# A two-layer cross-attention kernel: context and dequantized weight split in natural layout and turned by DMA, V projected before K on six banks, row constants added in the last stage

## The chip, the cores and the metric

The kernel runs on one NeuronCore of a Trainium2 chip. The time is the device time of one execution in microseconds (us). The engines are TensorE (PE in the rows; PEld is its weight load), VectorE (DVE), ScalarE (ACT), GpSimd (POOL) and SyncE (SP), which only issues transfers. Each runs its own list of instructions in order and waits at semaphores. PSUM has eight banks of 128 x 512 float32.

## What is computed

x is 2 x 512 x 1024 (eight tiles of 128 tokens), the context 2 x 1024 x 1024 (sixteen tiles). Four residual steps, each on a layer norm of x:

```python
x = x + tanh(g_xattn[0]) * matmul(fake_quant(ln(x)), fake_quant(ctx))            # A
x = x + tanh(g_ffn[0])   * (quant_per_token(ln(x)) @ dequant(W_int, scale).T + bias)  # B
x = x + tanh(g_xattn[1]) * attention(ln(x), ctx, ctx, Wq, Wk, Wv) @ Wo           # 32 heads, 8 K/V heads of 32
x = x + tanh(g_ffn[1])   * (ln(x) @ dequant_fp4(packed, scales).T)               # F
```

fake_quant(v) is (clip(round(v/s + z), 0, 255) - z) * s. Step A is done on integers shifted by 128, exact in float16; the two zero points come back as a term per token (c1, from the row sums of the quantized x) and a term per column (c2, from the column sums of the quantized context). A term that is constant along a row drops out of every later layer norm.

The K, V, Q and output projections work in float32 accuracy: each factor is split into a float16 high part and a float16 rest, and three products are summed (hi*hi, hi*lo, lo*hi).

## The kernel before, in words

**Stage 1, chunks.** The context is taken in four chunks of four tiles. A tile is loaded into one of four slots `cx`; TensorE turns it in float32 (`ctx_turn`, line 1264, eight 128 x 128 transposes into banks 0 and 1); ScalarE copies the turned halves to float16 (`ctx_high`, line 616), VectorE subtracts (`ctx_low`, line 899). GpSimd scales and clips the same slot for step A (`ctx_affine`, lines 451 and 453), VectorE rounds it into `r2` (`ctx_round`, line 905), which frees the slot for SP's next load. On TensorE a chunk c has two K projections (`k_proj`, 24 matmuls of 128 x 512 each) and four V projections (`v_proj`, 24 of 128 x 256) on banks 4 and 5 alone, and between them the turns of chunk c + 1, two turns of W's rows (`wd_turn`, into banks 2 and 3, with `wd_high`, `wd_low`), and the row sums c1 (`c1_sum`, line 1288, on bank 7). Beside it runs the first layer norm of two x tiles a chunk: statistics and affine on VectorE, `ln1_affine`, `ln1_round`, `ln1_out` between ScalarE and VectorE through one buffer y and one buffer r16, which SP turns by a DMA transpose (`xt1`, line 282). GpSimd adds c1 to x after it (`add_c1`, line 459, two tiles after each of the chunks 1, 2 and 3, the last two at the end), then c2 (`add_c2`, line 464).

**Stage 2, A and B.** `AB_OPS` sets the order: a0 to a4, b0, a5, b1, a6, b2, a7, b3 to b7, each on one of three pairs of banks. VectorE adds the product to x and takes statistics, ScalarE and VectorE quantize per token, SP turns the result (`xt2`, line 286). SP's list has two loads of Wq ahead of xt2(0), and they wait for GpSimd (`wq_low`, line 485), which comes to that after `add_c2` of all eight tiles. The third layer norm's scale and shift come in two groups of four tiles (`ln3_affine`).

**Stage 3, Q.** ScalarE writes the normalized tile and its high part (`y3_out`), GpSimd the rest, SP turns both (`xt3`, lines 290 and 292). Q is projected for batch 0 (eight blocks), then for batch 1, interleaved with the first score maxima (line 1410). In between VectorE unpacks the fp4 weight eight times (`unpack`, line 1139) into the one buffer r16, which SP turns into `w2T` (`w2_turn`, line 337); `q_low` (line 1124), for which TensorE's next Q block waits, stands behind it in VectorE's list.

**Stage 4** is the attention of 16 K/V groups; **stage 5** the output projection and step F, with stores from x.

## Time and profile before

| | us |
|---|---|
| median of 3 runs (lowest, highest) | 961.75 (957.26, 962.38) |
| the profiled execution's own time | 963.96 |
| its span, first to last instruction | 962.0 |
| TensorE busy | 859.1 (89% of the span) |
| VectorE, ScalarE, GpSimd busy | 595.2, 443.0, 556.5 |
| mean granted TensorE clock | 0.966 |

A busy share is a mean over stages. The stages lie as follows in the span, by TensorE's instructions: stage 1 from 24.3 us (its first projection) to 170.8, stage 2 to 267.7, stage 3 to 389.5, stage 4 to 818, stage 5 to the end. In stages 4 and 5 the change touches one thing only, the constant c1.

### The profile page before, as it was taken

Reading aid. Unit: us, or ns where it says so; the run is one execution under the profiler, and the core shown is the slowest. Engines: PE = TensorE matmul, PEld = TensorE weight load, DVE = VectorE, ACT = ScalarE, POOL = GpSimd, SP = SyncE. Lnnn points to the kernel's source line nnn. Section 1 sums busy time; section 2 is a strip of 40 time slices with the busy share of each in tenths; the row PEclk is TensorE's granted clock in tenths of the full one; section 3 lists DMA queues with packets and bytes.
Section 4 is the critical chain, followed back from the end, with each engine's and each line's share of the span. In section 5 each row is a group of like instructions: output and inputs, shape, how many; then the busy total and the mean of one; then the engine's idle time right before and its main releaser. Section 6 shows DMA issues by size and latency. Waiting matters only on the chain.

```text
span 962.0 us, 14337 instructions
## 1 busy us (share of the span) xinstructions
PE 859.1 (89%) x4592; PEld 341.2 (35%) x4592; DVE 595.2 (62%) x842; ACT 443.0 (46%) x740; POOL 556.5 (58%) x244
## 2 busy tenths in 40 slices
PE   3976779869985789799999999999999998999998
PEld 2645456424432334222222222222222221444443
DVE  4754365798823365577778777777778760155522
ACT  3343333544632110376667766777767767011000
POOL 4316246984635331178888888888888888321200
PEclk9998979979997989799999999999999999999999
DMA  4961522343377651144455445554445444222242
GB/s 171 359 175 37 161 56 76 88 105 93 61 185 148 181 142 44 53 91 98 94 118 118 96 102 113 118 118 107 101 98 109 101 88 82 50 44 44 55 131 76
DMA packets 102649, 103.09 MB, mean 107 GB/s; under 512 B 67152, under 2 KB 87632, under 8 KB 98512
## 3 DMA queue, kind: packets, MB, share of 16 engines
q1 hardware_dynamic: 98000, 68.97, 26.2%
q0 software_dynamic: 4608, 33.56, 17.3%
q8 instruction: 27, 0.44, 0.2%
q14 instruction: 14, 0.11, 0.0%
HBM read 41.55 MB, written 12.58 MB: 56 GB/s over the span
## 4 chain that ended last, share of the span: by engine, by line
PE 55%; DVE 16%; DMA 6%; issue 6%; POOL 4%; DVEq 4%; ACT 3%; POOLq 2%; SPq 2%; ACTq 1%
PE sbank L1456 10%; PE sbank L1465 10%; PE mpair L1410 9%; DVE mx L1152 5%; DVEq L857 3%; PE sbank L1542 3%; PE sbank L1557 3%; PE sbank L1546 3%; PE sbank L1559 3%; PE sbank L1544 3%; PE sbank L1297 3%; PE sbank L1298 3%; PE sbank L1299 3%; DMA regK<-r 2%; POOL X L464 2%
## 5 line engine op out<-in xcount | busy, mean ns | idle before, releaser
L1152 DVE TENSOR_REDUCE mx<-mpair 128x1 f32<-128x1024 f32 x256 | 301.3, 1216 | 82.1 <-PE mpair L1410 81.9
L803 ACT ACTIVATE regC<-sbank 128x512 f32<-128x512 f32 x512 | 279.5, 595 | 129.6 <-PE sbank L1456 128.0
L1456 PE MATMUL sbank<-regD 98*128 98x512 f16 x512 | 179.6, 388 | 9.3 <-DMA regD<-mT 5.1
L1410 PE MATMUL mpair<-regD 96*128 96x512 f16 x512 | 157.0, 384 | 7.8 <-DVE mx L1152 3.2
L553 POOL TENSOR_TENSOR wraw<-regC 128x2048 f32<-128x2048 f32 x32 | 145.2, 4537 | 24.5 <-ACT regC L803 12.4
L1465 PE MATMUL sbank<-regC,regD 128*32 128x512 f32 x1024 | 137.2, 608 | 1.0 <-ACT regC L803 1.0
L1456 PEld LDWEIGHTS sbank<-regD 98*128 98x128 f16 x512 | 46.6, 97 | 202.0 <-ACT regC L803 164.3
L553 POOL TENSOR_TENSOR regD<-regC 128x2048 f32<-128x2048 f32 x16 | 72.8, 4551 | 52.9 <-ACT regC L803 52.8
L553 POOL TENSOR_TENSOR tail<-regC 128x2048 f32<-128x2048 f32 x16 | 76.7, 4795 | 0.8 <-ACT regC L803 0.8
L1410 PEld LDWEIGHTS mpair<-regD 96*128 96x128 f16 (+1 forms) x512 | 49.3, 99 | 59.9 <-DVE mT L1162 10.6
L1297 PE MATMUL sbank<-xT_hi,regC 128*128 128x512 f16 x128 | 51.5, 403 | 20.3 <-DVE tail L1124 15.9
L459 POOL TENSOR_SCALAR X<-X,c 128x1024 f32<-128x1024 f32 x8 | 29.6, 3700 | 49.3 <-ACT c L646 49.3
L483 POOL TENSOR_SCALAR wraw<-wraw 128x1024 f32<-128x1024 f32 x16 | 17.2, 1075 | 64.9 <-ACT regR L746 31.3
L1298 PE MATMUL sbank<-xT_lo,regC 128*128 128x512 f16 x128 | 51.3, 401 | 0.0
L1299 PE MATMUL sbank<-xT_hi,regC 128*128 128x512 f16 x128 | 51.2, 400 | 0.0
L591 POOL TENSOR_TENSOR tail<-y,r 128x1024 f16<-128x1024 f32 x8 | 17.0, 2126 | 56.4 <-ACT r L844 56.4
L1264 PE MATMUL mpair<-id,xT_lo 128*128 128x128 f32 x128 | 22.1, 330 | 30.8 <-DVE regC L899 26.6
L1542 PE MATMUL sbank<-regR,xT_hi 128*128 128x512 f16 x128 | 48.5, 379 | 0.0
L1557 PE MATMUL sbank<-regK,xT_hi 128*128 128x512 f16 x128 | 48.5, 379 | 0.0
L1544 PE MATMUL sbank<-regR,xT_hi 128*128 128x512 f16 x128 | 48.5, 379 | 0.0
L1546 PE MATMUL sbank<-regR,xT_lo 128*128 128x512 f16 x128 | 48.5, 379 | 0.0
L1559 PE MATMUL sbank<-regK,xT_lo 128*128 128x512 f16 x128 | 48.5, 379 | 0.0
(165 smaller groups left out, 1318.3 us busy)
## 6 DMA issues: line engine op xcount, KB each, us to landing
regD<-wraw POOLq DMA_DIRECT2D x16, 1024.0 KB, 7.0
tail<-wraw POOLq DMA_DIRECT2D x16, 1024.0 KB, 7.0
xT_lo<-in_ctx SPq DMA_DIRECT2D x16, 512.0 KB, 5.4
wraw<-in_L_ffn_W_int SPq DMA_DIRECT2D x8, 512.0 KB, 6.5
wraw<-in_L_xattn_Wq SPq DMA_DIRECT2D x8, 512.0 KB, 3.7
wraw<-in_L_xattn_Wo SPq DMA_DIRECT2D x8, 512.0 KB, 4.1
regD<-q_hi_scratch SPq DMA_DIRECT2D x32, 128.0 KB, 2.5
out<-X SPq DMA_DIRECT2D x16, 256.0 KB, 2.0
```

Source lines behind the costliest of these rows:

```text
L553: nc.gpsimd.tensor_tensor(p_sum[pr if pr < 3 else 1][:, :, :], probs[:, (2 * pr) % 4, :, :], probs[:, (2 * pr) % 4 + 1, :, :], ALU.add).th ...
L803: nc.scalar.activation(probs[:, kt % 4, h, :], bank[4 + h % 2], ACT.Exp, scale=SCALE).then_inc(s["exp_ok"], 1)
L1152: v.tensor_reduce(mx[m][:, bass.ds(n, 1)] if par is not None else mx[m][:, n:n + 1], slot[:, :, :], AX.XY, ALU.max).then_inc(s["mx_red"], 1)
L1297: pe.matmul(dst, whi(k), xhi(k), start=(k == 0), stop=False)
L1298: pe.matmul(dst, whi(k), xlo(k), start=False, stop=False)
L1299: m = pe.matmul(dst, wlo(k), xhi(k), start=False, stop=(k == KD - 1))
L1410: m = pe.matmul(mpair[slot][:, half, :], qst[par][0:96, bass.ds(n * P, P)], kst[par][0:96, half * 512:(half + 1) * 512], start=True, stop= ...
L1456: pe.matmul(bank[4 + h % 2], kst[par][0:98, kt * P:(kt + 1) * P], qst[par][0:98, h * 512:(h + 1) * 512], start=True, stop=True).then_inc(s ...
L1465: m = pe.matmul(bank[6][HD * h:HD * h + HD, :], vst[par][:, kt * HD:(kt + 1) * HD], probs[:, kt % 4, h, :], start=(kt == 0), stop=(kt == K ...
L1542: pe.matmul(bank[4 + h], xT_hi[:, k, bass.ts(t, P)], wo_hi[:, k, h * H2:(h + 1) * H2], start=(k == 0), stop=False)
L1544: pe.matmul(bank[4 + h], xT_hi[:, k, bass.ts(t, P)], wo_lo[:, k, h * H2:(h + 1) * H2], start=False, stop=False)
L1546: m = pe.matmul(bank[4 + h], xTl[:, k, bass.ts(t, P)], wo_hi[:, k, h * H2:(h + 1) * H2], start=False, stop=(k == KD - 1))
```

## The change

- **Context.** The tile is split where it lies, in natural layout: `ctx_high` is one 128 x 1024 copy to float16 on ScalarE, `ctx_low` one 128 x 1024 subtraction on VectorE, into two buffers each (`nat_hi`, `nat_lo`, in the room of X tiles 6 and 7). SP turns both by DMA transposes (`ctx_turn`, 32 in all). GpSimd's scaling of a slot waits for `ctx_lo`.
- **W.** After `wd_scale` the same: high part on ScalarE, rest on GpSimd, two buffers, 16 DMA transposes (`wd_turn`). Chunk 1 has one W tile, chunk 2 two, the last chunk five.
- **Projections.** TensorE has nothing else in stage 1 but V on banks 0 to 3, then K on banks 4 and 5, and in the last chunk the column sums (banks 6 and 7).
- **c1.** The row sum is a by-product of `ln1_out` (`accum_out`), all eight constants come from one small VectorE instruction, ScalarE adds them to x behind `y_high` in stage 5 (lines 942 and 943), and `f_out` waits for that (`x_c1`). The matmuls of `c1_sum` and GpSimd's `add_c1` are gone. `add_c2(t)` waits until the first layer norm has read tile t.
- **Start.** Wv is loaded ahead of Wk; the six scalars are loaded from ScalarE's queue. X tiles 6 and 7 are loaded only when the last context transpose has landed.
- **Stages 2 and 3.** Four groups of two tiles in `ln3_affine`; y3 of tiles 0 to 5 ahead of the first Q block, 6 and 7 behind blocks 0 and 1. `unpack` has two buffers (`w2b`), and the first waits for the transposes of tiles 4 to 7 instead of 0 to 3.

```diff
+            def ctx_turn(u):
+                cols = bass.ds((u // TB % 2) * 512 + (u % TB) * P, P)
+                if u >= 2 * TB:
+                    sp.wait_ge(s["kv_mm"], 6 * (u // TB - 1))
+                sp.wait_ge(s["ctx_hi"], u + 1)
+                sp.dma_start_transpose(ctxT_hi[:, :, cols], nat_hi[u % 2]).then_inc(cth[u % 2], 16)
+                sp.wait_ge(s["ctx_lo"], u + 1)
+                sp.dma_start_transpose(ctxT_lo[:, :, cols], nat_lo[u % 2]).then_inc(ctl[u % 2], 16)
+
+            def wd_turn(w):
+                if w == 0:
+                    sp.wait_ge(s["wkv_lo"], 4)
+                sp.wait_ge(s["wd_hi_ok"], w + 1)
+                sp.dma_start_transpose(wd_hi[:, :, bass.ts(w, P)], wnat_hi[W_BUF[w]]).then_inc(wdh[W_BUF[w]], 16)
+                sp.wait_ge(s["wd_lo_ok"], w + 1)
+                sp.dma_start_transpose(wd_lo[:, :, bass.ts(w, P)], wnat_lo[W_BUF[w]]).then_inc(wdl[W_BUF[w]], 16)
+                if w < KD - 2:
+                    load_wint(w + 2)
 
...
+            for c in range(NCH - 1):
+                u = TB * (c + 1)
+                ctx_turn(u)
+                if c == 0:
+                    load_ctx(7)
+                else:
+                    store_k(c - 1)
+                ctx_turn(u + 1)
+                if c == 0:
+                    load_wint(0)
+                    load_wint(1)
+                    sp.dma_start(X[:, 2:4, :], x_v[:, 2:4, :]).then_inc(x_in[1], 16)
+                if u + TB < U:
+                    load_ctx(u + TB)
+                ctx_turn(u + 2)
+                if c > 0:
+                    wd_turn(c - 1)
+                if u + TB < U:
+                    load_ctx(u + TB + 1)
+                store_v(c)
+                ctx_turn(u + 3)
+                if u + TB < U:
+                    load_ctx(u + TB + 2)
                 xt1(2 * c)
-                if c < NCH - 1:
-                    store_v(c)
-                    next_wint(c)
-                else:
-                    for k in range(2):
-                        sp.wait_ge(s["wd_tr"], 2 * (KD - 2 + k) + 2)
...
+            store_k(NCH - 2)
+            wd_turn(3)
+            wd_turn(4)
+            store_v(NCH - 1)
+            wd_turn(5)
+            xt1(T - 2)
+            wd_turn(6)
+            load_w(wq_v, 0, 0)
+            wd_turn(7)
+            load_w(wq_v, 1, 1)
+            xt1(T - 1)
+            store_k(NCH - 1)
```


ScalarE and VectorE in a chunk, TensorE's list and the last stage:

```diff
+            def ctx_high(u):
+                act.wait_ge(cin[u % TB], 16 * (u // TB + 1))
+                if u >= 2:
+                    act.wait_ge(cth[u % 2], 16 * (u // 2))
+                    act.wait_ge(s["ctx_lo"], u - 1)
+                nc.scalar.activation(nat_hi[u % 2], cx[:, u % TB, :], ACT.Copy).then_inc(s["ctx_hi"], 1)
...
+            def chunk(c, first=False):
+                u = TB * (c + 1)
+                ctx_high(u)
+                v_out(c, 0, first)
+                ctx_high(u + 1)
+                ln1_root(c)
+                v_out(c, 1, first)
+                ctx_high(u + 2)
+                if c > 0:
+                    wd_high(c - 1)
+                v_out(c, 2, first)
+                ln1_affine(2 * c)
+                v_out(c, 3, first)
+                ctx_high(u + 3)
+                ln1_out(2 * c)
+                if c == 2:
+                    wd_high(2)
+                ln1_affine(2 * c + 1)
                 k_out(c, 0, first)
-                ctx_part(0)
-                ln_sd(2 * c, 2, s["ln1_stat"], c + 1, s["ln1_sd"])
-                if not first:
-                    c1_out(2 * c - 2)
+                ln1_out(2 * c + 1)
                 k_out(c, 1, first)
-                if not first:
...
+            def ctx_low(u):
+                dve.wait_ge(s["ctx_hi"], u + 1)
+                if u >= 2:
+                    dve.wait_ge(ctl[u % 2], 16 * (u // 2))
+                v.tensor_tensor(nat_lo[u % 2], cx[:, u % TB, :], nat_hi[u % 2], ALU.subtract).then_inc(s["ctx_lo"], 1)
+
...
+            def chunk(c):
+                u = TB * (c + 1)
+                ctx_low(u)
                 if c == 1:
                     dve.wait_ge(x_in[1], 32)
-                stats(2 * c, 2 * c)
-                stats(2 * c + 1, 2 * c + 1).then_inc(s["ln1_stat"], 1)
-                d()
-                round_part(0)
+                ln1_stats(c)
+                ctx_low(u + 1)
+                if c > 0:
+                    wd_scale(c - 1)
+                ctx_round(u)
+                ln1_affine(c)
+                ctx_low(u + 2)
+                ctx_round(u + 1)
+                ln1_round(2 * c)
+                if c == 2:
+                    wd_scale(2)
+                ctx_low(u + 3)
+                ctx_round(u + 2)
+                k_low(c, 0)
+                ln1_round(2 * c + 1)
...
                 nc.scalar.activation(y_hi, y[:, :], ACT.Copy).then_inc(s["y_hi"], 1)
+                if first:
+                    act.wait_ge(s["c1_ok"], 1)
+                nc.scalar.activation(X[:, t, :], X[:, t, :], ACT.Identity,
+                                     bias=c1[:, bass.ds(t, 1)]).then_inc(s["x_c1"], 1)
```


```diff
                 else:
-                    dve.wait_ge(s["w2_tr"], 16 * w)
-                dst = r16[:, :].rearrange("p (b j e) -> p b j e", b=NB4, e=2)
+                    if w >= 2:
+                        dve.wait_ge(w2_tr[w % 2], 16 * (w // 2))
+                dst = w2b[w % 2].rearrange("p (b j e) -> p b j e", b=NB4, e=2)
                 for e in range(2):
...
+            dve.wait_ge(xt3_hi[1], 16 * TB)
+            dve.wait_ge(xt3_lo[1], 16 * TB)
             for n in range(6):
                 unpack(n, n == 0)
                 q_low(0, n + 2, n % 2)
...
             for c in range(NCH):
-                chunk(c, first=(c == 0), more=(c < NCH - 1))
+                for j in range(TB):
+                    v_proj(c, j)
+                if c == NCH - 1:
+                    c2_sum(0)
+                    c2_sum(1)
+                k_proj(c, 0)
+                if c == NCH - 1:
+                    c2_sum(2)
+                    c2_sum(3)
+                k_proj(c, 1)
 
```


How this moves instructions. First ScalarE, one chunk (c = 1) before; regC is the turned context, regD the turned W, tail the K pair, r the quantized x, X and vtmp as named:

```order
L653 ACTIVATE tail<-sbank 128x512
L616 ACTIVATE regC<-mpair 128x4x128 x2
L627 ACTIVATE sd<-mv,sc 128x2
L646 ACTIVATE c<-sbank,sc 128x1
L653 ACTIVATE tail<-sbank 128x512
L646 ACTIVATE c<-sbank,sc 128x1
L616 ACTIVATE regC<-mpair 128x4x128 x2
L659 ACTIVATE vtmp<-sbank 128x8x32
L634 ACTIVATE y<-X,bb,rr 128x1024
L616 ACTIVATE regC<-mpair 128x4x128 x2
L622 ACTIVATE regD<-mpair 128x4x128 x2
L659 ACTIVATE vtmp<-sbank 128x8x32 x2
L641 ACTIVATE r<-y,sc 128x1024
```


and after (X now holds the split context, tail also the split W):

```order
L682 ACTIVATE X<-xT_lo 128x1024
L722 ACTIVATE vtmp<-mpair 128x8x32
L682 ACTIVATE X<-xT_lo 128x1024
L695 ACTIVATE sd<-mv,sc 128x2
L722 ACTIVATE vtmp<-mpair 128x8x32
L682 ACTIVATE X<-xT_lo 128x1024
L691 ACTIVATE tail<-wraw 128x1024
L722 ACTIVATE vtmp<-mpair 128x8x32
L702 ACTIVATE y<-X,bb,rr 128x1024
L722 ACTIVATE vtmp<-mpair 128x8x32
L682 ACTIVATE X<-xT_lo 128x1024
L709 ACTIVATE r,c<-y,sc 128x1024
L702 ACTIVATE y<-X,bb,rr 128x1024
```


Between two chunks' first casts stood the copies out of the turns; now each cast is a single instruction ahead of the V copies (line 722), and `ln1_out` of the chunk before (the line-709 row that follows a K copy) stands ahead of the next chunk's first cast.

Second SP, the same chunk before:

```order
L221 DMA xT_lo<-in_ctx 128x1024 x3
L261 DMA k_hi_scratch<-tail 128x2x512
L262 DMA k_lo_scratch<-tail 128x2x512
L221 DMA xT_lo<-in_ctx 128x1024
L282 DMA_TRANSPOSE xT_hi<-r 128x8x128
L268 DMA v_scratch<-vtmp 128x8x128
L234 DMA wraw<-in_L_ffn_W_int 128x1024 x2
L282 DMA_TRANSPOSE xT_hi<-r 128x8x128
```


and after, the start of it:

```order
L254 DMA_TRANSPOSE regC<-X 128x8x128
L238 DMA xT_lo<-in_ctx 128x1024
L252 DMA_TRANSPOSE regC<-X 128x8x128
L254 DMA_TRANSPOSE regC<-X 128x8x128
L260 DMA_TRANSPOSE regD<-tail 128x8x128
L262 DMA_TRANSPOSE regD<-tail 128x8x128
L245 DMA wraw<-in_L_ffn_W_int 128x1024
L238 DMA xT_lo<-in_ctx 128x1024
L277 DMA v_scratch<-vtmp 128x8x128
L252 DMA_TRANSPOSE regC<-X 128x8x128
L254 DMA_TRANSPOSE regC<-X 128x8x128
L238 DMA xT_lo<-in_ctx 128x1024
```


On SP's queue stand eight context transposes and two of W for each chunk beside the two of x (line 285), in one list with the loads.

Third SP in stage 3, before, from the load of Wo to the second turn of the unpacked weight (regK is its turned form, r the buffer); lines 332 and 333 store Q, lines 350 to 355 stage a K/V group:

```order
L278 DMA wraw<-in_L_xattn_Wo 128x1024 x2
L337 DMA_TRANSPOSE regK<-r 128x8x128
L332 DMA q_hi_scratch<-tail 128x512
L333 DMA q_lo_scratch<-tail 128x512
L350 DMA regD<-q_hi_scratch 32x4x512 x2
L350 DMA regD<-q_lo_scratch 32x4x512
L353 DMA regD<-k_hi_scratch 32x1024
L353 DMA regD<-k_lo_scratch 32x1024
L353 DMA regD<-k_hi_scratch 32x1024
L355 DMA regD<-v_scratch 128x256
L337 DMA_TRANSPOSE regK<-r 128x8x128
```


and after, from the same load to the same turn (lines 387 and 388 store Q):

```order
L281 DMA wraw<-in_L_xattn_Wo 128x1024 x2
L387 DMA q_hi_scratch<-tail 128x512
L388 DMA q_lo_scratch<-tail 128x512
L392 DMA_TRANSPOSE regK<-r 128x8x128
L387 DMA q_hi_scratch<-tail 128x512
L388 DMA q_lo_scratch<-tail 128x512
L392 DMA_TRANSPOSE regK<-regD 128x8x128
```


Between the first two turns of the unpacked weight stood a store of Q and the seven loads of a staging; now stands one store, and the two turns read two buffers, r and regD.

## Rows read from the trace of the kernel before

**Rows 1.** windows: us, busy (instructions) of each engine, clock, DMA share, GB/s
```profile
24.30:55.20 30.90, 29.02 (x193) 19.79 (x194) 21.27 (x36) 15.22 (x25) 11.30 (x9) 1.00 0.81 294
55.20:97.80 42.60, 29.24 (x209) 21.01 (x209) 20.46 (x37) 13.88 (x27) 17.09 (x10) 0.92 0.38 112
97.80:140.90 43.10, 31.60 (x208) 21.86 (x208) 20.45 (x37) 13.67 (x27) 16.85 (x10) 0.84 0.38 104
140.90:170.80 29.90, 29.89 (x208) 19.38 (x209) 16.09 (x27) 12.35 (x22) 18.21 (x7) 1.00 0.32 84
170.80:200.50 29.70, 18.02 (x98) 8.06 (x96) 25.07 (x42) 14.71 (x17) 28.69 (x12) 0.88 0.48 117
200.50:267.70 67.20, 67.15 (x304) 29.98 (x304) 56.14 (x97) 33.00 (x32) 41.62 (x23) 0.98 0.35 80
267.70:331.40 63.70, 46.45 (x193) 19.87 (x194) 20.87 (x34) 17.22 (x20) 24.10 (x14) 0.87 0.69 170
331.40:389.50 58.10, 51.85 (x225) 22.26 (x222) 32.85 (x39) 8.67 (x12) 13.58 (x9) 0.94 0.35 98
```

**Rows 2.** what TensorE waited for, 0 to 260 us: total, times, longest
```profile
PE mpair L1264 <- DVE regC L899: 26.6, 5, 7.9
PE mpair L1390 <- DMA xT_hi<-r: 10.2, 1, 10.2
```

**Rows 3.** timeline, stage 1: start, us, engine, line, operation, [idle before]
```profile
38.81 0.27 PE L1297 MATMUL sbank<-regK,regC 128*128 128x256 f16 x1
...
41.44 1.04 PE L1264 MATMUL mpair<-id,xT_lo 128*128 128x128 f32 x8
...
64.38 1.15 ACT L641 ACTIVATE r<-y,sc 128x1024 f16<-128x1024 f32 x1 [8.84 <-DMA xT_hi<-r]
...
71.51 7.40 POOL L459 TENSOR_SCALAR X<-X,c 128x1024 f32<-128x1024 f32 x2 [17.91 <-ACT c L646]
...
81.32 0.69 DVE L905 TENSOR_SCALAR regR<-xT_lo 128x1024 f16<-128x1024 f32 x1 [10.48 <-POOL xT_lo L453]
...
83.72 1.54 DVE L911 SCALAR_TENSOR_TENSOR wraw<-wraw,wscale 128x1024 f32<-128x1024 int32 x1
...
88.40 1.22 DVE L911 SCALAR_TENSOR_TENSOR wraw<-wraw,wscale 128x1024 f32<-128x1024 int32 x1
```

**Rows 4.** groups by line and form, 0 to 200 us: busy us, mean ns, idle
```profile
L464 POOL TENSOR_TENSOR X<-X,xT_lo 128x1024 f32<-128x1024 f32 x8 | 21.0, 2654 | 0.3
...
L888 DVE SCALAR_TENSOR_TENSOR regK<-regD,regK 128x1024 f16<-128x1024 f32 x4 | 5.3, 1323 | 3.0 <-ACT regK L606 3.0
...
L485 POOL TENSOR_TENSOR regC<-wraw,regC 128x1024 f16<-128x1024 f32 x2 | 4.3, 2126 | 0.3
...
L606 ACT ACTIVATE regK<-regD 128x1024 f16<-128x1024 f32 x4 | 4.2, 1055 | 4.3 <-DMA regD<-in_L_xattn_Wv 2.8 <-DMA regD<-in_L_xattn_Wk 1.5
```

**Rows 5.** landing of line 282's transposes; two on SP's queue; DMA from 58.2 to 69.0
```profile
DMA to landing us min/median/max: 3.1/4.6/6.1
...
262.65 1.33 SPq L292 DMA_TRANSPOSE xT_lo<-regR  x1
264.03 1.33 SPq L290 DMA_TRANSPOSE xT_hi<-regR  x1
...
GB/s 137 273 341 379 372 383 379 421 432 311 319 319 217 326 250 157 111 89 260 295 329 343 355 341 338 425 381 455 455 349 425 440 455 349 342 273 199 59 289 143
DMA packets 4201, 3.38 MB, mean 313 GB/s; under 512 B 2224, under 2 KB 3760, under 8 KB 4201
```

**Rows 6.** what TensorE, then VectorE waited for, 250 to 410 us
```profile
PE sbank L1297 <- DVE tail L1124: 15.9, 3, 10.1
PE sbank L1297 <- DMA xT_lo<-regR: 4.4, 1, 4.4
...
DVE r L1139 <- DMA regK<-r: 33.5, 5, 12.7
```

**Rows 7.** the page's 40 slices of the span: ACT
```profile
ACT  3343333544632110376667766777767767011000
```

641 lines of the change are left out of this document (309 added, 332 removed).

## The prediction

> **What bounds the kernel now.** I read the windows first [rows 1]: chunks 1 and 2 of stage 1 take 42.6 and 43.1 us, and in them no engine is full: TensorE 29 and 32 us, VectorE 20, GpSimd 17, the transfers 0.38. A V projection takes 41.44 - 38.81 = 2.63 us [rows 3], K with twice the columns 5.2, so four V and two K need 21 us; the rest of TensorE's time is turns, row sums and the lower clock. Where nothing is full, a circle of waits sets the pace, and the waits show it. TensorE's turns of the context waited 26.6 us for VectorE's subtraction [rows 2]. VectorE stood 10.5 us ahead of a rounding, for GpSimd; GpSimd had spent 7.4 us on two additions of c1, and had waited 17.9 us for that c1; ScalarE had stood 8.8 us for the one buffer r to be turned [rows 3]. So c1 (x quantized, turned, summed, added) delays the next chunk's context and with it K's store and the next projection.
>
> Stage 2 is TensorE's from 200.5 on: 67.15 busy of 67.2 us [rows 1]. Ahead of it b0 stands 10.2 us for its transposed tile [rows 2]. Stage 3 takes 63.7 + 58.1 = 121.8 us [rows 1] for 16 blocks of 5.2 and 16 score products of two matmuls, some 7 us together: 90. The other 32 are waits and slow clock (0.87 and 0.94 granted): TensorE waited 15.9 us for `q_low` and 4.4 for the transposes of y3, and `q_low` stood behind `unpack`, which waited 33.5 us for the one buffer r [rows 6].
>
> **Stage 1 after.** Out of TensorE go the turns of context and W and the row sums; 21 us a chunk are left, so TensorE stops being near the bound. Out of GpSimd go eight additions of 3.7 us, 29.6 us. What comes in is 48 DMA transposes on SP's queue. In a row they are issued 1.38 us apart [rows 5]; alone one lands in 3.1 to 6.1 us, median 4.6 [rows 5]. Each brings 256 KB, 190 GB/s at 1.38 us. The trace doesn't show many of them among loads. Bounds: 0.7 us, if they ran like a plain load of that size in its best moments (0.256 MB at some 380 GB/s), and 2.2 us: from 58.2 to 69.0 us the transfers moved 3.38 MB with two of them, and if the other 2.86 MB went at the 455 GB/s of the best slice, 6.3 us, the two had 4.5 [rows 5]. I take 1.4, the row that is nearest.
>
> The Trainium skill (Advanced Engine Details and Errata, section X-Bar Transpose (TRN2)) says that such transposes are as fast as regular DMAs, 350 to 400 GB/s; the 1.38 us of this trace contradict it by a factor of two. By that rule the circle below would be some 5 us shorter, which is the low rival.
>
> Is it bandwidth or a circle? A middle chunk now moves 12 transposes (8 context, 2 W, 2 x) of 1.4, and loads and stores of 3.5 MB, some 10 us at 350 GB/s: 27 of transfer time. The circle is longer. From the first cast of a chunk to the next chunk's: cast 1.1 (line 606's 1.055 for 128 x 1024 [rows 4]); then VectorE's list up to the third subtraction: subtraction 1.3 (line 888 [rows 4], the nearest two-input pass), statistics 3.1 (four of 0.7 and the sums, an estimate), subtraction 1.3, W scaling 1.2, rounding 0.7, affine 3.2 (88.40 - 83.72 less the 1.5 of the W scaling [rows 3]), subtraction 1.3: 12.1. Then SP: the third tile's low turn 1.3, W's high turn 1.3, the wait for GpSimd's rest of W (line 485, 2.1 [rows 4]), 4.7 in all; W's low turn, two loads, V's store, the fourth tile's two turns, a load: 5.5; then the transpose of x, issued behind some 5 us of transfers: 8 to landing. ScalarE's `ln1_out` of the second x tile waits for that, because r is one buffer, and it stands ahead of the next chunk's first cast: 1.2, and K's copy 0.6. Sum 33.2 us, against 43 now. DVE and ACT passes of the new forms I price by these rows though no row shows two SBUF operands with a float16 result at 128 x 1024 but line 888; between 1.1 and 1.7 each.
>
> Start: the first V projection now needs one tile's turns and Wv. A V at 19 us (between 13, if nothing stood in the queue, and today's 24.3); the fourth V waits for tile 3's turns and ends at 34. Then a circle a chunk: the last V of chunk 3 ends at 34 + 3 x 33 = 133. Behind it: column sums 3.5, K 5.2, a wait of 7 for ScalarE's copy of the column sums (in its list behind W's casts and the layer norm of x tiles 6 and 7, whose load now starts last), sums 3.5, K 5.2, and 1.6 of clock: a0 at 159, today 170.8.
>
> From a0 to b0 today 29.7 us. After: GpSimd has six tiles of `add_c2` left at 2.65, W's last rest 2.1 and two `wq_low` of 3.3 ([rows 4], line 485 and its scaling), ahead of which SP doesn't issue xt2(0); that ends near 185, then issue and landing 4.6: b0 at 190, today 200.5. Gain at b0: 10 us. From there TensorE is full as today. VectorE gets two more `ln3_affine` of some 3.5 us, and has 67.2 - 56.1 = 11 us free [rows 1], so I cost that at nothing; without the cover it would be 3.
>
> **Stage 3 after.** y3 of tiles 0 to 5 comes while TensorE runs b4 to b7 (27 us), so the 4.4 us wait and some 2.4 us at the lower clock behind it go. Then the new wait: `unpack` now stands for tile 7. From Q's start: block 1 ends at 10.4, y3(7) 2.4, rest 2.1, turns 4.6: 20; unpack 2.3 and `q_low` 0.7 (estimates by line 888): 23. Block 4 could start at 20.8: 2.2 us of wait in place of the 10.1 us one [rows 6]. After that a turn of w2 is issued on its own buffer two blocks (10 us) ahead of its use, and lands in 5: no wait. Of today's 32 us some 5 stay: gain 27.
>
> **Stage 5.** Eight additions of c1 on ScalarE, 1.2 us each, where ScalarE is at 0 to 1 tenths [rows 7]; a tile there takes over 10 us. Nothing. If ScalarE's adding to a sum in `ln1_out` costs, it is within 0.5 us a tile, 1 a chunk.
>
> **Sum.** 10 + 27 = 37 us off the profiled execution's own 963.96: 927. The median of the runs lies 2.2 lower, so 925.
>
> **Rivals.**
> - *Transposes slow beside loads (the other side).* At 2.2 us each, 12 a chunk: the queue alone is 12 x 2.2 + 10 = 36 us, and the circle gets some 5 us longer at its waits for landings; over start, three circles and the ten W turns of the tail b0 comes at about 216: 952. At 2.45 us b0 is 27 us late and all that stage 3 gives is used up; beyond, slower: at 2.8, 975 to 985. For: the busy share was 1.08 from 58 to 69 us with only two among the loads; against: 1.38 in a row [rows 5].
> - *Stage 1 gives nothing.* The circle over r and SP's order stays at 40 instead of 33: b0 at today's place, 937. For: SP has 12 x 1.33 and some ten short issues, about 20 us, a chunk.
> - *Stage 3 gives half.* The wait for tile 7 and the turns queued behind stores come back as 10 to 14 us: 939. Against: two blocks of slack.
> - *Low rival: transposes at plain rate*, 0.7 us each, and little queueing: the circle is 28, b0 at 175, 910. Against: 1.38 us each [rows 5]. The rule of the Trainium skill above would make it so.
>
> **Chances.** Forecast 925 (range 915 to 934) 0.42; stage 1 gives nothing or stage 3 half (935 to 945) 0.25; slow transposes, faster still by over 0.5% (945 to 957) 0.10, no change 0.04, slower 0.06; low rival (under 915) 0.13. Range 906 to 950, which leaves out some 2 in 10. Faster by over 0.5% (4.8 us, about what a measurement of this kernel can tell from no change) 0.90, same 0.04, slower 0.06.
>
> **What would show it.** Right: TensorE's first V near 19 us, chunks 31 to 36 us apart, a0 near 159, b0 near 190, ScalarE idle some 10 us a chunk ahead of `ln1_out` for a transpose of x; from b7's end to the last Q block some 95 us, with one wait of about 2 us at block 4; stage 4 and 5 of the same length. Wrong: the landing of context transposes above 8 us with the DMA share near 1.0 in stage 1 (slow transposes); a wait at block 4 of 10 us; TensorE busy throughout stage 1 (then the circle isn't there and the time is below 910).

## The result, and the profile after

| | before | after |
|---|---|---|
| median, us (lowest, highest) | 962.01 (957.26, 962.38) | 953.89 (951.98, 955.09) |
| the profiled execution's own time | 963.96 | 955.09 |
| its span | 962.0 | 953.5 |

The ratio is 0.9929 with a 95% interval of 0.9904 to 0.9954, so the change is faster by 8 us where 37 were forecast; the range of the prediction ended at 950. The stages of the changed kernel, with windows cut at the like places (V comes first now, so a chunk ends with its last V: the first V at 17.6 us; the ends of the last V of the four chunks at 35.0, 65.8, 103.6 and 137.6; then a0, b0, the end of b7, the second batch of Q). Columns: window, its length, busy us (instructions) of TensorE, its weight loads, VectorE, ScalarE and GpSimd, granted clock, DMA share, GB/s:

```profile
17.60:35.00 17.40, 14.36 (x97) 11.13 (x98) 9.39 (x9) 4.50 (x5) 13.55 (x8) 0.91 1.12 271
35.00:65.80 30.80, 23.93 (x146) 15.20 (x144) 15.60 (x25) 9.44 (x13) 11.75 (x8) 0.88 1.06 265
65.80:103.60 37.80, 23.87 (x146) 15.18 (x144) 19.67 (x28) 14.20 (x22) 14.80 (x9) 0.82 0.97 221
103.60:137.60 34.00, 23.78 (x145) 15.15 (x144) 23.41 (x30) 13.22 (x21) 17.73 (x10) 0.85 0.83 168
137.60:165.40 27.80, 18.89 (x80) 8.04 (x79) 13.28 (x21) 11.56 (x17) 11.93 (x6) 0.87 1.01 221
165.40:197.50 32.10, 19.31 (x81) 8.09 (x79) 27.71 (x44) 14.99 (x16) 29.47 (x15) 0.87 0.58 146
197.50:265.80 68.30, 68.27 (x304) 30.27 (x304) 59.38 (x108) 33.26 (x34) 39.01 (x21) 0.96 0.33 74
265.80:318.80 53.00, 44.23 (x193) 19.25 (x193) 28.59 (x36) 17.00 (x20) 25.64 (x16) 0.94 0.88 209
318.80:380.50 61.70, 53.34 (x225) 22.41 (x223) 34.25 (x38) 8.55 (x12) 14.54 (x10) 0.92 0.35 91
```

Against [rows 1]: a0 comes at 165.4 instead of 170.8, b0 at 197.5 instead of 200.5, b7 ends at 265.8 instead of 267.7, and the last block of Q at 380.5 instead of 389.5. Stages 4 and 5 take 573.0 us, and 572.5 before. So 3 us came from stage 1, where TensorE is idle for 7 to 14 us of every window behind the first, 1 us was lost again in stage 2, and 7 came from stage 3. The transfers are now at 0.83 to 1.12 of their time through stage 1; [rows 1] had 0.38 in the two middle chunks.

What TensorE waited for up to 400 us (us in total, times, longest):

```profile
PE mpair L1380 <- DMA regC<-X: 41.4, 5, 17.6
PE mpair L1380 <- issue: 10.3, 5, 6.2
PE mpair L1456 <- DMA xT_hi<-r: 10.3, 1, 10.3
PE sbank L1415 <- ACT xT_lo L742: 8.9, 1, 8.9
PE sbank L1380 <- DMA xT_lo<-regR: 7.0, 1, 7.0
PE mpair L1472 <- DVE mx L1267: 6.7, 3, 3.9
PE sbank L1380 <- DVE tail L1238: 3.4, 3, 1.6
```

The first line answers to the 26.6 us of [rows 2]: a projection that waits for a turned tile of context, now for its DMA (17.6 of the 41.4 is the start). The third is the old wait ahead of b0, unchanged. The 7.0 ahead of Q answers to the 4.4 of [rows 6], and the waits on `q_low` (15.9 there) are down to 3.4. In their place stands VectorE's maximum, 6.7.

The traffic of SP's queue, before and then after (packets, MB, share of 16 engines' span):

```profile
q1 hardware_dynamic: 98000, 68.97, 26.2%
```
```profile
q1 hardware_dynamic: 147840, 81.56, 35.3%
```

That is 252.0 us of 962.0 before and 336.6 of 953.5 after, so 84.6 us of packet time for 48 transposes, 1.76 us each; in a row they were 1.38 apart [rows 5]. The packet times of transfers that run side by side are added up (the first windows above stand at 1.12 and 1.06), so 1.76 is what a transpose adds to that sum, not how long one lasts.

### The profile page after: what moved, and what is told of

The parts are those of the page before. It is cut to its first block, busy times and chain, and to the rows that moved or that the text cites. A ratio compares the mean times of both kernels' runs of the same rounds, so it can differ in the third digit from the quotient of the medians.

```text
span 953.5 us, 13888 instructions
## 1 busy us (share of the span) xinstructions
PE 838.8 (88%) x4336; PEld 317.7 (33%) x4336; DVE 608.0 (64%) x823; ACT 448.1 (47%) x726; POOL 552.8 (58%) x243
## 4 chain that ended last, share of the span: by engine, by line
PE 51%; issue 15%; DVE 9%; POOL 8%; POOLq 5%; DMA 4%; DVEq 2%; SPq 2%; ACT 1%; ACTq 1%
PE sbank L1518 10%; PE sbank L1527 10%; PE mpair L1472 9%; DVE mx L1267 5%; POOLq L500 3%; PE sbank L1604 3%; PE sbank L1621 3%; PE sbank L1606 3%; PE sbank L1619 3%; PE sbank L1608 3%; DVEq L956 2%; POOL xT_lo L501 2%; PE sbank L1537 2%; POOL regC L543 2%; POOLq L542 2%
## 5 line engine op out<-in xcount | busy, mean ns | idle before, releaser
L1472 PE MATMUL mpair<-regD 96*128 96x512 f16 x512 | 158.1, 386 | 11.1 <-DVE mx L1267 6.7
L1380 PE MATMUL mpair<-regK,regC 128*128 128x256 f16 x128 | 39.8, 311 | 51.7 <-DMA regC<-X 41.4
L1472 PEld LDWEIGHTS mpair<-regD 96*128 96x128 f16 (+1 forms) x512 | 49.2, 99 | 64.3 <-DVE mT L1277 10.6
L499 POOL TENSOR_SCALAR xT_lo<-xT_lo,sc 128x1024 f32<-128x1024 f32 x16 | 30.4, 1902 | 65.9 <-DVE X L998 49.7
L1380 PE MATMUL sbank<-xT_hi,regC 128*128 128x512 f16 x128 | 51.1, 399 | 10.4 <-DMA xT_lo<-regR 7.0
L541 POOL TENSOR_SCALAR wraw<-wraw 128x1024 f32<-128x1024 f32 x16 | 17.8, 1112 | 54.2 <-ACT regR L835 25.5
```

What stands on the lines that cost most here:

```text
L1380: pe.matmul(dst, whi(k), xhi(k), start=(k == 0), stop=False)
L1472: m = pe.matmul(mpair[slot][:, half, :], qst[par][0:96, bass.ds(n * P, P)], kst[par][0:96, half * 512:(half + 1) * 512], start=True, stop= ...
```

## The circle in stage 1, read from the trace after

The stretch 81 to 103 us of chunk 2, timeline rows of ScalarE, then GpSimd, then SP's queue (start, us, engine, line, operation, [idle before]):

```profile
82.33 1.14 ACT L709 ACTIVATE r<-y,sc 128x1024 f16<-128x1024 f32 x1
...
101.55 1.15 ACT L709 ACTIVATE r<-y,sc 128x1024 f16<-128x1024 f32 x1 [16.18 <-DMA xT_hi<-r]
...
85.14 2.12 POOL L508 TENSOR_TENSOR tail<-wraw,tail 128x1024 f16<-128x1024 f32 x1
...
81.03 1.23 SPq L254 DMA_TRANSPOSE regC<-X  x1
82.36 1.29 SPq L260 DMA_TRANSPOSE regD<-tail  x1
87.28 1.23 SPq L262 DMA_TRANSPOSE regD<-tail  x1
...
90.20 4.56 SPq L252 DMA_TRANSPOSE regC<-X  x1
94.80 1.37 SPq L254 DMA_TRANSPOSE regC<-X  x1
96.21 0.58 SPq L238 DMA_DIRECT2D xT_lo<-in_ctx  x1
96.83 1.24 SPq L285 DMA_TRANSPOSE xT_hi<-r  x1
```

ScalarE had the quantized x of tile 2 ready in r at 83.5. SP could issue its transpose (L285) only at 96.8: it had stood 3.6 us for GpSimd's low half of W (L508, done at 87.26), then went through a load, a store and the fourth context tile's turns, the first of which took 4.6 us to issue instead of 1.3, in a stretch (90 to 95 us) in which the transfers stood at 1.00 of their time. GpSimd itself was late with L508 by its own passes over the context: the two ahead of it took 2.09 and 1.82 us, the like two of the chunk's first tile 1.20 and 1.04.

```profile
81.11 2.09 POOL L499 TENSOR_SCALAR xT_lo<-xT_lo,sc 128x1024 f32<-128x1024 f32 x1 [2.09 <-DVE X L998]
83.35 1.82 POOL L501 TENSOR_SCALAR xT_lo<-xT_lo 128x1024 f32<-128x1024 f32 x1 [0.15 <-issue]
```

ScalarE's next rounding into the one buffer r waited 16.2 us for the landing at 101.5, and the next chunk's first cast (L682) stands behind it. That is the circle of the prediction, at 35.1 us (first casts at 68.0 and 103.2) where 33.2 were forecast. TensorE stands beside it: it waited 10.8 us for the fourth tile, and its V projection behind that ran at a granted clock of 0.50 (the lower of the two levels, 1.2 GHz) and took 5.1 us (98.29 to 103.36), where a V at the full clock takes 2.6.

## The experiments

Each was timed on the same chip as runs of the kernel before, whose median was 958.8 to 960.5 in these five groups; the changed kernel was timed beside a kernel before of 962.0 and not again. So differences between rows of under some 3 us are not told from the times alone, and the stages of the profiles have to show them. Where the stages lie in each profiled execution, by TensorE's instructions (us; "b7-Q" is the stretch from the end of b7 to the end of the last block of Q):

| kernel | time | ratio to before (95%) | a0 | b0 | b0 to b7's end | wait ahead of Q | Q batch 0 | Q batch 1 | b7-Q |
|---|---|---|---|---|---|---|---|---|---|
| before | 962.0 | | 170.8 | 200.5 | 67.2 | 4.4 | 59.2 | 58.2 | 121.8 |
| after | 953.9 | 0.993 (0.990 to 0.995) | 165.4 | 197.5 | 68.3 | 7.0 | 46.0 | 61.7 | 114.7 |
| b_c1 | 933.2 | 0.972 (0.968 to 0.976) | 152.6 | 170.3 | 69.6 | 6.8 | 59.0 | 55.3 | 121.0 |
| b_stage3 | 960.4 | 1.000 (0.998 to 1.002) | 169.3 | 198.9 | 68.8 | 6.6 | 49.4 | 62.6 | 118.6 |
| b_c1_s3 | 927.5 | 0.965 (0.963 to 0.968) | 153.1 | 170.8 | 70.7 | 8.6 | 45.6 | 59.6 | 113.8 |
| e_wo_first | 943.8 | 0.983 (0.979 to 0.986) | 165.8 | 197.7 | 68.7 | 6.4 | 45.6 | 51.5 | 103.5 |
| e_y3_dve | 949.9 | 0.989 (0.985 to 0.993) | 166.8 | 198.8 | 67.3 | 0.9 | 49.8 | 59.8 | 110.5 |
| e_two_r | 943.3 | 0.982 (0.980 to 0.984) | 156.8 | 188.8 | 68.5 | 6.6 | 46.3 | 61.7 | 114.6 |
| e_plain | 948.4 | 0.987 (0.985 to 0.990) | 159.3 | 191.4 | 68.4 | 6.5 | 46.3 | 61.8 | 114.6 |
| e_wd_late | 941.1 | 0.980 (0.977 to 0.982) | 154.9 | 187.1 | 67.2 | 7.7 | 44.8 | 60.9 | 113.3 |
| e_xt2_first | 951.1 | 0.989 (0.985 to 0.992) | 167.5 | 191.0 | 72.5 | 8.5 | 46.2 | 60.5 | 115.2 |
| e_all | 926.0 | 0.965 (0.962 to 0.968) | 153.3 | 176.8 | 73.6 | 0.7 | 50.5 | 49.4 | 100.6 |
| b_best | 915.1 | 0.953 (0.951 to 0.955) | 153.3 | 171.1 | 70.7 | 2.1 | 50.7 | 48.6 | 101.3 |
| b_wdma | 933.0 | 0.971 (0.967 to 0.975) | 161.7 | 183.3 | 72.5 | 1.5 | 49.5 | 49.5 | 100.6 |

Names that begin with b_ start from the kernel before (turns on TensorE), those with e_ from the changed kernel.

### Parts of the change alone: b_c1, b_stage3, b_c1_s3

b_c1 is the kernel before with this part of the diff:

```diff
-                nc.scalar.activation(r16[:, :], y[:, :], ACT.Identity, bias=NMZ).then_inc(s["ln1_ready"], 1)
+                nc.scalar.activation(r16[:, :], y[:, :], ACT.Identity, bias=NMZ,
+                                     accum_out=c1[:, t:t + 1]).then_inc(s["ln1_ready"], 1)
...
-            def c1_out(t):
...
-            def add_c1(t):
...
-            def c1_sum(t):
...
+                nc.scalar.activation(X[:, t, :], X[:, t, :], ACT.Identity,
+                                     bias=c1[:, bass.ds(t, 1)]).then_inc(s["x_c1"], 1)
```

> The kernel before with the c1 part of the change alone: the sum of x comes out of ScalarE's rounding (accum_out), TensorE's sums and GpSimd's eight additions are gone, and c1 is added to X in the last stage. Theory 1 (my first reading of the waits, that GpSimd's wait of 17.9 us for c1 and its 7.4 us of additions delay the next chunk's context): chunks 1 to 3 get 5 to 9 us shorter each, b0 comes near 180 to 190 instead of 200.5, and the time falls by 10 to 20 us, which is more than the whole change gave. Theory 2 (the circle in stage 1 goes over the one buffer r and its transposes, and c1 hangs beside it): b0 within 3 us of 200.5, time within 4 us of before.

Measured: 933.2, 26 us under before and 21 under the whole change. Three of its windows: the two middle chunks (cut at the starts of K), and from a0 to b0:

```profile
54.60:86.80 32.20, 28.57 (x193) 20.27 (x194) 20.19 (x37) 13.23 (x27) 8.94 (x8) 0.95 0.51 147
86.80:119.10 32.30, 27.10 (x193) 19.14 (x194) 20.22 (x37) 13.17 (x27) 9.98 (x8) 1.00 0.57 139
152.60:170.30 17.70, 17.43 (x82) 7.70 (x79) 14.89 (x30) 9.20 (x10) 12.86 (x7) 1.00 0.66 180
```

The two middle chunks went from 42.6 and 43.1 us [rows 1] to 32.2 and 32.3, with TensorE still turning everything. GpSimd is down from 17 to 9 or 10 us. And from a0 to b0 it takes 17.7 instead of 29.7 us, since GpSimd, free of the additions, comes to `wq_low` sooner (4 us behind a0 instead of 18; TensorE waits 0.3 us ahead of b0 instead of 10.2). Theory 1 holds, and everything goes beyond its upper end: 10 to 11 us a chunk, b0 at 170.3, 26 us in the time. The part takes out TensorE's sums, ScalarE's copies of them and GpSimd's additions at once; which of the three was worth how much was not separated.

b_stage3 is the kernel before with the stage 3 part only, that is `Y3_HI`, `ln3_affine` in pairs, the order of SP's list, and

```diff
-                sp.dma_start_transpose(w2T[:, :, bass.ts(w, P)], r16[:, :]).then_inc(s["w2_tr"], 16)
+                sp.dma_start_transpose(w2T[:, :, bass.ts(w, P)], w2b[w % 2]).then_inc(w2_tr[w % 2], 16)
```

> The kernel before with the stage 3 part of the change alone (y3 in new buffers, statistics of y3 two tiles at a time, two buffers for the unpacked W2, the new order of stores and turns). Theory 1 (the parts add up, and stage 3 gave its own 7 us of the 8 that the change gave): Q starts some 7 us after b7, the first batch of Q takes about 46 us, the second about 61, and the time is 955 to 957. Theory 2 (what stage 3 lost was taken by stage 1's late work, such as transposes and loads still under way): the wait ahead of Q is at most 4.4 us and the second batch takes 58, so the time is below 950.

Measured: 960.4, no difference. Between b7 and the last block of Q it saves 3.2 us in the profile; the second batch of Q takes 62.6 instead of 58.2, as in the changed kernel. The time misses both theories, and batch 0 took 49.4 us where theory 1 had 46. The trace decides for theory 1 all the same: the wait ahead of Q (6.6) and the long second batch come with the stage 3 part whatever stage 1 does.

b_c1_s3 has both parts, by the two diffs above, and lacks the DMA turns, the order of the projections and the order of the first loads that goes with them.

> The c1 part and the stage 3 part of the change together, on the kernel before: the whole change but for the DMA transposes of context and W and the new order of the projections (TensorE still turns both). Theory 1 (the DMA transposes took back what the c1 part gives; the stage 3 part gives little where its waits come back as others): 928 to 934, so 20 to 26 us faster than the changed kernel, b0 at 170 to 173 as with the c1 part alone. Theory 2 (the c1 part alone was fast because stage 3 happened to fall well): 940 or more, b0 late too.

Measured: 927.5, so the stage 3 part gives 6 us once the c1 part is there. DMA turns, with the new order of projections and first loads, made the kernel 26 us slower than the rest of the change made it, and theory 1 holds (0.5 us under its range): b0 at 170.8 with TensorE's turns, at 197.5 with DMA's. No run has the new order without the DMA turns, so the 26 us are those of all three together.

### Stage 3: e_wo_first, e_y3_dve

In SP's list of stage 3, here and at three other places:

```diff
-                w2_turn(6 + n)
                 next_wo(6 + n)
+                w2_turn(6 + n)
                 store_q(1, n, n)
```

> The changed kernel with four places exchanged in SP's list of stage 3: the load of a block of Wo is issued ahead of the turn of W2 beside it, not behind it. Theory 1 (the second batch of Q runs in a circle: unpack, turn issued, load of Wo issued behind it and landing 4.5 us later, ScalarE's cast of Wo, the copy of Q behind that cast in ScalarE's list, q_low on VectorE, next unpack): the waits of 2.7 and 3.9 us in the second batch and its slow matmuls go, it takes 50 to 53 us instead of 61.7, and the time falls by 7 to 11 us against the changed kernel, to 943 to 947. Theory 2 (VectorE's list is too long there, with unpack slowed by GpSimd beside it): no more than 2 us.

Measured: 943.8, the second batch in 51.5 us instead of 61.7. The rows of the changed kernel that gave the reason (VectorE, then SP's queue, then ScalarE, then TensorE):

```profile
334.49 1.35 DVE L1254 SCALAR_TENSOR_TENSOR r<-regR,scale 128x512 f16<-128x512 int32 x2
...
343.17 0.69 DVE L1238 SCALAR_TENSOR_TENSOR tail<-sbank,tail 128x512 f16<-128x512 f32 x1 [4.88 <-ACT tail L872]
...
335.87 1.24 SPq L392 DMA_TRANSPOSE regK<-r  x1
337.15 0.57 SPq L281 DMA_DIRECT2D wraw<-in_L_xattn_Wo  x1
...
341.60 1.06 ACT L835 ACTIVATE regR<-wraw 128x1024 f16<-128x1024 f32 x1 [10.50 <-DMA wraw<-in_L_xattn_Wo]
342.56 0.58 ACT L872 ACTIVATE tail<-sbank 128x512 f16<-128x512 f32 x1
...
347.39 1.03 PE L1472 MATMUL mpair<-regD 96*128 96x512 f16 x2 [3.87 <-DVE mx L1267]
```

`unpack` ends at 335.84, only then SP issues the turn and behind it the load of Wo (337.15), ScalarE's cast of Wo waits for it until 341.60, the copy of Q (L872) stands behind that cast, `q_low` (L1238) and the next `unpack` behind the copy, and the maxima that TensorE waits for behind that. The load had no need to wait for `unpack`. Exchanging two lines at these four places opened the circle, as theory 1 says.

In e_y3_dve GpSimd's part loses two tiles and VectorE's list gets them ahead of `ln3_affine(2)`:

```diff
-            for t in range(2, 6):
+            for t in range(4, 6):
                 y3_low(t)
...
+            for t in (2, 3):
+                dve.wait_ge(s["y3_hi"], t + 1)
...
+                v.tensor_tensor(y3_lo[t], ys[t % 2], y3_hi[t], ALU.subtract).then_inc(s["y3_lo"], 1)
```

> The changed kernel with the subtractions for the low halves of y3 of tiles 2 and 3 on VectorE instead of GpSimd. Theory 1 (the 7.0 us ahead of Q are GpSimd's list: add_bias and wq_low of 6 and 7 stand ahead of y3_low(2)): the wait falls to 0 to 2 us, Q starts at 266 to 268, the time falls by 5 to 8 us. Theory 2 (VectorE is as full there, its small operations take 1.9 to 2.2 us beside GpSimd, and 2.4 us more delay b6 and b7): Q starts at 270 or later, the time falls by under 3 us.

Measured: 949.9, 4 us less, between the two theories; the intervals of the two ratios overlap, but from b7's end to the last Q block the profile has 4.2 us less too. The wait ahead of Q went from 7.0 to 0.9 and Q starts at 267.1, as theory 1 says. What it missed is that 3.8 us came back inside batch 0 (49.8 instead of 46.0): Q starts 5.7 us earlier and then stands 6.75 us at block 4 for `q_low`, behind `unpack`, which waits for tile 7, just the wait that the prediction had put there. It is three times as long as forecast for a reason that the queue of this run shows (SP's rows; L383 loads the packed fp4 weight, 2 MB, 10.1 us to landing):

```profile
275.98 0.58 SPq L383 DMA_DIRECT2D regD<-in_L_ffn_weight_packed  x1
...
279.85 6.09 SPq L295 DMA_TRANSPOSE xT_lo<-regR  x1
...
288.37 1.32 SPq L295 DMA_TRANSPOSE xT_lo<-regR  x1
```

Behind that load the low turn of tile 6 took 6.09 us to issue. Tile 7's low half was ready at 282.7, its turn was issued at 288.4 and had landed at 291.5: 8.8 us where the prediction had 4.6. e_all shows the same, 6.15 us behind the same load. That the load holds the issue up is read from the order of the rows; no run moves it.

GpSimd's list in the changed kernel:

```profile
258.21 2.35 POOL L550 TENSOR_TENSOR X<-X,tail 128x1024 f32<-128x1024 f32 x1
260.52 1.05 POOL L541 TENSOR_SCALAR wraw<-wraw 128x1024 f32<-128x1024 f32 x1
261.71 2.13 POOL L543 TENSOR_TENSOR regC<-wraw,regC 128x1024 f16<-128x1024 f32 x1
263.80 2.12 POOL L554 TENSOR_TENSOR regR<-vtmp,regR 128x1024 f16<-128x1024 f32 x1
```

The last of these is `y3_low(2)`, whose high half was ready at 253.6. It stood behind `add_bias` and `wq_low` of 6 and 7, from 252.6 on.

### Stage 1, the changed kernel: e_two_r, e_plain, e_wd_late, e_xt2_first

```diff
+        R_BUF = [0, 1, 0, 1, 0, 0, 0, 0]
+        rL = [r16[:, :], r2[:, U - 1, :]]
...
-                nc.scalar.activation(r16[:, :], y[:, :], ACT.Identity, bias=NMZ,
+                nc.scalar.activation(rL[R_BUF[t]], y[:, :], ACT.Identity, bias=NMZ,
```

> The changed kernel with a second buffer for the quantized x of tiles 1 and 3 (the row of r2 that is written last), so that ScalarE's rounding of these two needs no landed transpose. Theory 1 (my prediction's circle: cast, subtractions, SP's queue, transpose of x, rounding over the one buffer r, next cast): ScalarE's waits of 13.4 and 16.2 us ahead of that rounding fall to under 5, chunks 2 and 3 get 5 to 9 us shorter each, b0 comes 8 to 15 us earlier, the time is 940 to 946. Theory 2 (the circle is SP's queue and the transposes' own transfer time; the buffer only shows it): the wait moves to the next cast or projection and b0 gains 0 to 4 us, the time is 950 to 954.

Measured: 943.3, b0 8.7 us earlier. ScalarE's waits for the buffer fell from 37.2 us to 7.3, but TensorE's wait for the fourth tile of chunk 2 stayed at 11.1 us, and only the one of chunk 3 fell, from 9.9 to 3.1. Theory 1 has the time and, at its lower end, the gain at b0; of the two chunks that it makes shorter only chunk 3 is (26.5 us instead of 34.0, last V to last V; chunk 2 stays at 37.5). There the next thing in the same queue is late once the buffer isn't.

```diff
-                sp.dma_start_transpose(ctxT_hi[:, :, cols], nat_hi[u % 2])
+                sp.dma_start(ctxT_hi[:, :, cols], nat_hi[u % 2].rearrange("p (k n) -> p k n", k=KD))
...
```

and so for the other three kinds of turns. This kernel leaves the turning out: K, V and step B are computed from operands that are not transposed, so its result is not that of the program; it is there for its time.

> The changed kernel with the 48 DMA transposes of context and W made plain copies of the same bytes between the same buffers, in 256-byte pieces: nothing is turned, so K, V and stage 2 compute with untransposed operands. Theory 1 (the transposes' own rate, 1.76 us each beside loads, costs the stage): the busy share of the transfers in stage 1 falls, issues on SP take no 2 to 5 us, the last V of chunk 3 ends at 115 to 125 instead of 137.6, the time is 935 to 942. Theory 2 (the length of the chain of waits, with SP's order, costs it): the last V ends at 130 or later, the time is 947 or more.

Measured: 948.4, the last V of chunk 3 at 132.2. Both numbers are in theory 2's range: cheaper transfers gave 5.5 us. The queue's packet time is 33.9% of 947.7 = 321.3 us, so a plain copy adds (321.3 - 252.0) / 48 = 1.44 us in 256-byte pieces, and the copies were hardly a cheap stand-in. ScalarE still waited 35.0 us for transposes of x (37.2 in the changed kernel). The order of waits holds the chunk with these slightly cheaper transfers too; what transfers of half the price would do was not run.

```diff
                 ctx_turn(u + 2)
-                if c > 0:
-                    wd_turn(c - 1)
...
                 xt1(2 * c)
+                if c > 0:
+                    wd_turn(c - 1)
```

> The changed kernel with W's turns of chunks 1 and 2 issued behind the fourth tile's turns and the first transpose of x in SP's list, not ahead of them. Theory 1 (SP stands there 4 to 5 us a chunk for GpSimd's low half of W, with the fourth context tile already split since 6 to 8 us): the waits of 10.8 and 9.9 us ahead of the last V of chunks 2 and 3 fall by 4 to 8 us each, b0 comes 6 to 12 us earlier, the time is 942 to 948. Theory 2 (the transfers' own backlog, 1.0 of their time in that stretch, sets the landing): b0 gains under 3 us, 951 to 954.

Measured: 941.1, b0 10.4 us earlier, the largest single gain in stage 1, and in the time 1 us more than theory 1 allowed: TensorE's waits of 10.8 and 9.9 us for the fourth tile fell to 4.9 and 1.5. All of it is order; the transposes are as many as before.

```diff
-            next_wq(2)
-            next_wq(3)
             xt2(0)
+            next_wq(2)
             xt2(1)
+            next_wq(3)
```

> The changed kernel with the transposes for b0 and b1 issued ahead of the loads of blocks 2 and 3 of Wq. Theory 1 (the 10.3 us ahead of b0 are SP's place behind a load that waits for GpSimd: tile 0 was ready at 185.6 and was issued at 192.9): b0 starts at 190 to 192, and some of it lasts: 946 to 950. Theory 2 (VectorE, 30 of 33 us busy from 165 to 198, sets stage 2's later tiles, so TensorE only waits elsewhere): the wait ahead of b0 falls, but the time stays at 951 to 954.

Measured: 951.1, in theory 2's range, and its interval overlaps that of the changed kernel, so at most a few us. From a0 to b0 it takes 23.5 instead of 32.1 us, but stage 2 takes 72.5 instead of 68.3 with a new wait of 5.2 us for VectorE's X. b0 comes at 191.0, as theory 1 says, and little of it lasts, as theory 2 says.

### Together: e_all, b_best

e_all is the changed kernel with the five edits above that keep the DMA turns (e_two_r, e_wd_late, e_xt2_first, e_wo_first, e_y3_dve).

> The changed kernel, turns by DMA as they are, with all five edits: second buffer for the quantized x, W's turns late in SP's list, transposes of b0 and b1 first, loads of Wo first, y3 of tiles 2 and 3 on VectorE. Theory 1 (the DMA turns themselves are cheap, it is their waits and places in one queue that cost): 918 to 926, near the 915 of the kernel with TensorE's turns. Theory 2 (what 48 transposes need of one queue and of the transfers keeps stage 1 long): 928 to 936.

Measured: 926.0, at the upper end of theory 1's range and 28 us under the changed kernel. b0 comes at 176.8. One by one the five edits gave 10.6, 12.8, 2.8, 10.1 and 4.0 us, 40 in all: they overlap, since one wait often stood under another.

b_best is b_c1_s3 with the edits of e_wo_first and e_y3_dve.

> The kernel of the run beside it (c1 part and stage 3 part, turns on TensorE) with the loads of Wo issued ahead of the turns of W2, and the subtractions for y3 of tiles 2 and 3 on VectorE. By the measured -10 and -4 us of these two edits on the changed kernel: 915 to 920. Rival (in the other stage 2, where b0 comes earlier and GpSimd is less behind, the y3 edit gives nothing or costs): 920 to 925.

Measured: 915.1, at the lower end of the expected range, which came from the two measured edits (927.5 - 10 - 4 = 913.5). With the five edits the kernel with DMA turns (e_all) is still 11 us behind this one with TensorE's, which has two of them only.

### What a transpose in the queue costs: b_wdma, b_wdma_late, b_spare, b_best_r, b_spare_r

| kernel | time | ratio to before (95%) | chunks 1 and 2, us |
|---|---|---|---|
| b_best | 915.1 | 0.953 (0.951 to 0.955) | 32.2, 32.1 |
| b_wdma | 933.0 | 0.971 (0.967 to 0.975) | 38.1, 36.6 |
| b_wdma_late | 929.2 | 0.968 (0.965 to 0.970) | 33.5, 31.9 |
| b_spare | 933.7 | 0.973 (0.970 to 0.975) | 41.0, 41.5 |
| b_best_r | 907.4 | 0.946 (0.944 to 0.948) | 28.6, 28.6 |
| b_spare_r | 922.3 | 0.960 (0.958 to 0.963) | 37.5, 36.8 |

b_wdma: in b_best, W is split in natural layout (on ScalarE and VectorE) and turned by DMA, the context stays with TensorE. One of the two buffers for the split parts is the room of the bias, so the bias is loaded and scaled later, and the loads of Wq stand behind W's last turns.

The first line is of TensorE's list, the others of SP's:

```diff
-                wd_turn(2 * c, 0, first)
...
+                wd_turn(2 * c)
                 xt1(2 * c)
                 store_v(c)
+                wd_turn(2 * c + 1)
                 xt1(2 * c + 1)
```

> The fastest kernel so far (c1 and stage 3 parts, turns on TensorE, loads of Wo first, y3 on VectorE: 915.1) with W alone split in natural layout and turned by 16 DMA transposes, context still by TensorE. Theory 1 (a chunk of 32.1 us is near TensorE's 30 busy us, so taking 3 us of turns a chunk from it helps, and SP has room): chunks of 29 to 31 us, 907 to 912. Theory 2 (the chunk's length comes from the chain context turn, cast, subtraction, GpSimd, next load, and more waits on SP): 913 to 920.

Measured: 933.0, and both theories are wrong: 18 us slower with 16 transposes and what moves with them. ScalarE waited 31.3 us for transposes of x in stage 1 (17.8 in b_best).

b_wdma_late:

```diff
-                wd_turn(2 * c)
                 xt1(2 * c)
+                wd_turn(2 * c)
                 store_v(c)
-                wd_turn(2 * c + 1)
                 xt1(2 * c + 1)
+                wd_turn(2 * c + 1)
```

> The kernel with W alone turned by DMA (933.0), with W's turns issued behind the transposes of x in SP's list instead of ahead. Theory 1 (its chunks of 38 us came from ScalarE's 14 us wait for the transpose of x over the one buffer r, which stood behind W's turns and a load): chunks of 32 to 34 us, 916 to 923. Theory 2 (the backlog of transfers behind W's turns sets it): 928 to 934.

Measured: 929.2. The chunks fell to 33.5 and 31.9 and ScalarE's wait to 18.5, as theory 1 says, but little of it reached the end, so the time is in theory 2's range. a0 comes at 152.7, as in b_best (153.3), and b0 at 180.9 instead of 171.1: the second block of Wq is loaded behind the last W turns (issued at 166.3), ScalarE waits 7.1 us for it, and the transpose of tile 0 for b0 is issued at 177.6 instead of 168.0. The order explains the chunks and, at another place of the queue, the tail.

b_spare adds transposes that nobody needs:

```diff
                         load_ctx(TB * c + 2 * TB + j, j)
+                        for n in range(12 * c + 3 * j, 12 * c + 3 * j + 3):
+                            spare_turn(n)
```

> The fastest kernel so far (turns on TensorE, 915.1) with 24 DMA transposes more, 12 each in two chunks of stage 1, three behind every load of context, from Wk's high half into rows that are written later; no engine waits for them but VectorE, long after. This prices what a dozen transposes a chunk take of SP's queue and of the transfers, without the waits of the change. Theory 1 (the change lost its 27 us to waits on landings and to places in SP's list, not to the occupied queue): at most 3 us, 915 to 918. Theory 2 (the queue and the transfers are the cost: some 16 us of SP's issue and 17 to 21 us of transfers a chunk): the two chunks get 4 to 8 us longer each, 923 to 932.

Measured: 933.7, 18.6 us more for 24 of them: theory 2, and beyond. SP's queue in its chunk 1, then ScalarE:

```profile
52.28 5.46 SPq L282 DMA_TRANSPOSE regR<-regK  x3
57.79 0.58 SPq L227 DMA_DIRECT2D xT_lo<-in_ctx  x1
58.41 5.03 SPq L282 DMA_TRANSPOSE regR<-regK  x3
63.49 0.58 SPq L267 DMA_DIRECT2D k_hi_scratch<-tail  x1
...
65.17 5.18 SPq L282 DMA_TRANSPOSE regR<-regK  x3
70.40 1.32 SPq L296 DMA_TRANSPOSE xT_hi<-r  x1
...
73.75 1.15 ACT L654 ACTIVATE r<-y,sc 128x1024 f16<-128x1024 f32 x1 [17.67 <-DMA xT_hi<-r]
```

And the same two places of b_best:

```profile
58.85 1.33 SPq L287 DMA_TRANSPOSE xT_hi<-r  x1
...
64.62 1.15 ACT L643 ACTIVATE r<-y,sc 128x1024 f16<-128x1024 f32 x1 [8.78 <-DMA xT_hi<-r]
```

Nine spare transposes hold the queue for 15.7 us, 1.74 each, so the transpose of x is issued at 70.4 instead of 58.9, and ScalarE stands 17.7 us instead of 8.8. No engine waits for the spare ones until long after. SP itself waits ahead of each for the landing of the fourth before it, which had always come by the end of the issue ahead, so that held nothing up. And yet they cost a chunk 9 us.

b_best_r is b_best with the second buffer of e_two_r (its diff is there), b_spare_r the same with the spare transposes of b_spare.

> The fastest kernel so far (turns on TensorE, 915.1) with a second buffer for the quantized x of tiles 1 and 3. Theory 1 (in its chunks of 32.2 us ScalarE stands 8.8 us for the transpose of x over the one buffer r, and the next casts behind it): chunks 1 and 2 get 1 to 3 us shorter, as TensorE with 30 busy us is the next bound: 910 to 913. Theory 2 (TensorE bounds it already): within 1 us of 915.

> The same with the 24 unneeded DMA transposes of before in SP's list. Theory 1 (they cost 18.6 us only by putting the transposes of x 11.6 us later in the queue, which ScalarE's rounding waits for over r; with the second buffer nobody waits for these so soon): within 5 us of the kernel beside it. Theory 2 (the occupied queue and the transfers hold something else as well, the loads of context first of all): 8 us or more above it.

Measured: 907.4 and 922.3. The second buffer is worth 8 us to b_best, more than theory 1 gave it (chunks of 28.6 us), and 907.4 is the fastest kernel of this study, 5.4% under before. The spare transposes still cost 15 us, theory 2. ScalarE now waits in another place:

```profile
66.99 0.60 ACT L665 ACTIVATE tail<-sbank 128x512 f16<-128x512 f32 x1 [9.99 <-DMA k_lo_scratch<-tail]
```

K's store is issued at 63.2, behind nine of them, and ScalarE's next copy of K needs its buffer (in b_best_r it waits 3.6 us there at most). Take one wait away and the next thing in the queue is late.

## Why the prediction was wrong

The forecast was 10 us from stage 1 and 27 from stage 3. Measured: 3.0 at b0, 1.1 lost in stage 2, 7.1 from stage 3.

**Stage 3, 20 of the 28 missing us, is the step that failed.** "Of today's 32 us some 5 stay: gain 27." From b7's end to the last Q block I forecast 95 us and it took 114.7. Of the 5 that stay only 2.2 have a term in the prediction.
- "the 4.4 us wait and some 2.4 us at the lower clock behind it go": it became 7.0. I let y3 of tiles 0 to 5 come while b4 to b7 ran, and did not write down GpSimd's list for that stretch, in which `y3_low(2)` comes behind 11 us of other work; its passes stood in [rows 4], at 2.1 to 2.7 us each. e_y3_dve shows the cause, and also that removing the wait gives only 4 us, because the next wait (block 4) was hidden under it.
- "2.2 us of wait in place of the 10.1 us one", at block 4: it was 1.0 in the changed kernel, where Q started 7 us late. In e_y3_dve and e_all, where Q starts on time, it is 6.7 and 6.8. The mechanism was right and its size a third of what it is. The term that was mis-sized is "turns 4.6" of tile 7, which took 8.8 behind the load of the packed weight (e_y3_dve); the 1.0 of the changed kernel is no support for the 2.2.
- "After that a turn of w2 is issued on its own buffer two blocks (10 us) ahead of its use, and lands in 5: no wait": the second batch of Q took 61.7 us where eight blocks of 5.2 and 7 us of score products make 48.6, and even longer than the 58.1 of before. I had followed the buffer and not the load of Wo that SP issues behind the turn. e_wo_first gives 10.2 of these 13.1 us back.

**Stage 1: the circle was right, two of its terms were not.** I had the last V at 133 and it was 137.6, a0 at 159 and it was 165.4, b0 at 190 and it was 197.5. The 7.5 us are 1.0 of the start, 3.6 of three chunks (some 2.5 of them the lower clock under the last V, 5.3 us long behind a wait of 9.9), 1.8 between the last V and a0, and 1.1 from a0 to b0. In the circle SP's list from the third tile's low turn to the transpose of x had 4.7 + 5.5 = 10.2 us in mine, and 96.83 - 81.03 = 15.8 in the trace of chunk 2: SP stood 3.6 us for GpSimd where I had 2.1, and the first turn behind took 4.56 us to issue where I had 1.3. The next term erred the other way: from the issue of x's transpose to ScalarE I had 8 us, and it was 4.7 (96.83 to 101.55). That the circle came out at 35.1 against 33.2 is in part luck. e_wd_late gives 10 us back at b0 by taking SP's stand out of the way.

**What I did not see at all is what the parts were worth.** I read that c1 delayed the next chunk [rows 3] and removed GpSimd's 29.6 us in my sum, but never asked what the kernel would do with that part alone. It gains 26 us (b_c1). The DMA turns, with the order of projections and first loads, then took 26 back (b_c1_s3 against the changed kernel). The forecast of 10 us in stage 1 was the difference of two large terms that I had not written down. That the turns alone are dear, b_wdma and b_spare make likely; what the order is worth by itself stays open.

**The rivals.** "Transposes slow beside loads" had the right sign of the error in stage 1, and 1.76 us lies between its 2.2 and my 1.4; its result, b0 at 216, did not come, and of its two signs only the busy transfers did: a context transpose landed in 4.0 us (median), not above 8. "Stage 1 gives nothing" named the circle over r and SP's order, and e_two_r and e_wd_late show that both hold stage 1, though the circle is 35 us and not 40; "stage 3 gives half" was nearer to stage 3 than the forecast. I had given 0.25 to one or the other and nothing to both, and both came: 953.9 fell into a band that I had kept for slow transposes. The low rival needed 0.7 us a transpose; they took 1.76, and even a plain copy of the same bytes in 256-byte pieces took 1.44, by the same measure.

**The rule of the Trainium skill** (Advanced Engine Details and Errata, section X-Bar Transpose (TRN2)) is that such transposes run as fast as regular DMAs, at 350 to 400 GB/s. The runs contradict it for these 256 KB tiles: in the kernel before, from 263 to 266 us, transposes alone had the transfers at 1.01 of their time and moved 195 GB/s. Nearer to it is the comparison with a plain copy in 256-byte pieces: the transpose's 1.76 us are 1.22 times its 1.44.

**The rest held.** The sum in `ln1_out`, for which the prediction had a bound of 0.5 us a tile and no row, took 0.19 us, in an instruction of its own behind the pass. c1 on ScalarE in stage 5 cost nothing that the stages show; stages 4 and 5 kept their length within 0.5 us. The two additional `ln3_affine` cost at most the 1.1 us by which stage 2 is longer.

## What to carry to other kernels

A DMA that nobody waits for still costs what stands behind it in the same queue (18.6 us for 24 of them in b_spare): before an operation moves from an engine with time to spare to a DMA queue, write down what that queue issues next and who waits for that. Price every part of a change by itself against the kernel before, since a gain and a loss of 26 us each look like a small gain. When a list is rewritten, each line of it is a place at which something else can come late, and exchanging two lines at four places (load ahead of the turn that waits) gave 10 us, more than the 8 of the whole change.

## What the hardware showed that I had not expected

Transposes of 128 x 1024 float16 hold the queue for 1.7 us each where loads are under way (5.46, 5.03 and 5.18 us for three in b_spare), against 1.33 in a row without loads [rows 5], and single ones for 4.56 us (the changed kernel) and 6.09 us (e_y3_dve) behind loads. So a long issue seems to tell of a backlog ahead of it; no run was made to show that alone.

Tiny operations of VectorE on two columns take 0.16 us while GpSimd is idle, and up to 2.2 beside GpSimd's passes over SBUF. Two rows of the changed kernel, the second while GpSimd adds the bias from 258.21 on (above):

```profile
248.58 0.16 DVE L1031 TENSOR_TENSOR ra<-ra,nhalf 128x2 f32<-128x2 f32 x1
...
258.34 2.23 DVE L1031 TENSOR_TENSOR ra<-ra,nhalf 128x2 f32<-128x2 f32 x1
```

Whether the two share a port or something else was not tried.
